# Queries projected three batches ahead in both attentions of a two-layer cross-attention kernel

## What is computed

```python
def _layernorm(x):
    m = jnp.mean(x, axis=-1, keepdims=True)
    v = jnp.var(x, axis=-1, keepdims=True)
    return (x - m) / jnp.sqrt(v + 1e-05)

# first attention, 16 heads of 16 numbers, no mask
q, k, v = heads(x0 @ Wq.T + bq), heads(ctx @ Wk.T + bk), heads(ctx @ Wv.T + bv)
out = softmax(-0.25 * q @ k.T) @ v                  # per head
attn0 = merge(out) @ Wp.T + bp
# second attention: rotary on queries and keys, and a mask
s = where(mask, neg, rope(q) @ rope(k).T)
attn1 = merge(softmax(s) @ v) @ Wo.T + bo

x = x + tanh(g_xattn[0]) * attn0(_layernorm(x), ctx)
x = x + tanh(g_ffn[0]) * ffn0(_layernorm(x))
x = x + tanh(g_xattn[1]) * attn1(_layernorm(x), ctx)
x = x + tanh(g_ffn[1]) * ffn1(_layernorm(x))
```

## Time and profile before

| | us |
|---|---|
| median of three runs | 790.41 |
| the profiled execution | 789.21 |
| its span, first to last instruction | 787.4 |
| TensorE busy | 682.1 (87%) |
| VectorE, ScalarE, GpSimd busy | 452.6, 334.4, 218.9 |
| step 0 of the first attention (30.82 to 44.72) | 13.90 |
| steps 1 to 5, each | 12.93 |
| steps 6 and 7 | 11.1 and 12.8 |
| step 8, the first of the second attention (to 387.00) | 24.4 |
| steps 9 to 12, each | 16.4 to 16.5 |
| steps 13, 14, 15 | 16.0, 11.5, 12.2 |

### The profile page before, as it was taken

How to read it: one execution, slowest core, us unless ns; L and a number is a source line. 1 busy time by engine, 2 the same in 40 slices (tenths; PEclk the granted TensorE clock), 3 DMA queues, 4 the chain that set the end, 5 groups by cost and what they waited for, 6 DMA issues and landing times.

```text
span 787.4 us, 13684 instructions
## 1 busy us (share of the span) xinstructions
PE 682.1 (87%) x5104; PEld 548.8 (70%) x5104; DVE 452.6 (57%) x919; ACT 334.4 (42%) x757; POOL 218.9 (28%) x200
## 2 busy tenths in 40 slices
PE   5889988999987637775999998999988899999998
PEld 4667655778864334443666665899976799999997
DVE  4758755110127465667467545545877777788713
ACT  3455655556641201113344555322227566555510
POOL 6635311000000500057254321000105545544500
PEclk9999999999998856998799999999999999999999
DMA  7865660670000223014334440400000455566313
GB/s 269 237 175 163 173 181 2 254 304 16 0 0 1 92 112 105 1 40 124 94 103 127 113 129 2 161 1 1 1 1 1 160 189 197 194 225 225 113 34 107
DMA packets 61479, 87.22 MB, mean 111 GB/s; under 512 B 17265, under 2 KB 50801, under 8 KB 60401
## 3 DMA queue, kind: packets, MB, share of 16 engines
q1 hardware_dynamic: 60624, 85.90, 34.1%
q10 hardware_dynamic: 800, 0.59, 0.2%
HBM read 63.54 MB, written 18.73 MB: 104 GB/s over the span
## 4 chain that ended last, share of the span: by engine, by line
PE 74%; DVE 11%; issue 6%; ACT 4%; POOL 3%; DMA 2%; ACTq 0%; DVEq 0%; POOLq 0%
PE ps L924 72%; DVE keep L1741 2%; DMA keep<-in_x 1%; ACT big L674 1%; DVE keep L1752 1%; PE ps L930 1%; POOL kbr L505 1%; ACT keep L684 1%; DVE keep L1734 1%; DVE keep L1749 1%; POOL vp L546 1%; PE ps L1400 1%; DVE mcol L1558 0%; DMA m_rows<-big 0%; ACT vp L674 0%
## 5 line engine op out<-in xcount | busy, mean ns | idle before, releaser
L924 PE MATMUL ps<-keep 128*128 128x120 bf16 (+9 forms) x517 | 83.9, 286 | 39.8 <-DVE keep L1741 30.8
L924 PEld LDWEIGHTS ps<-keep 128*128 128x128 bf16 (+2 forms) x517 | 42.2, 119 | 68.1 <-DVE keep L1741 43.8
L924 PE MATMUL ps<-thi,whi 128*128 128x256 f32 x256 | 73.8, 288 | 3.9 <-POOL tlo L603 2.1
L924 PE MATMUL ps<-thi,wlo 128*128 128x256 f32 x256 | 72.4, 283 | 0.0
L924 PE MATMUL ps<-tlo,whi 128*128 128x256 f32 x256 | 72.4, 283 | 0.0
L768 ACT ACTIVATE ps<-ps 128x256 f32<-128x256 f32 x128 | 47.6, 372 | 38.6 <-PE ps L924 38.6
L924 PE MATMUL ps<-qpair,kpair 98*77 98x256 f32 x256 | 57.9, 341 | 3.8 <-ACT big L674 2.2
L505 POOL TENSOR_TENSOR kbr<-khi,keep 128x616 fp32r<-128x616 f32 x32 | 40.9, 1300 | 65.9 <-PE ps L924 63.6
L837 ACT ACTIVATE att<-ps 128x512 f32<-128x512 f32 x48 | 28.6, 596 | 68.6 <-PE ps L924 68.3
L924 PE MATMUL ps<-xhi,phi 128*128 128x512 f32 x128 | 50.7, 396 | 2.9 <-ACT ps L768 2.9
L924 PEld LDWEIGHTS ps<-thi,whi 128*128 128x128 f32 x256 | 48.9, 191 | 5.8 <-issue 3.4
(11 more groups left out here) (219 smaller groups left out, 1812.0 us busy)
## 6 DMA issues: line engine op xcount, KB each, us to landing
qpair<-q_rows SPq DMA_DIRECT2D x16, 768.0 KB, 5.7
q_rows<-qhi SPq DMA_DIRECT2D x32, 256.0 KB, 2.7
big<-in_piw SPq DMA_DIRECT2D x4, 2048.0 KB, 12.4
q_rows<-qlo SPq DMA_DIRECT2D x16, 256.0 KB, 2.7
att<-in_wg SPq DMA_DIRECT2D x8, 512.0 KB, 3.6
att<-in_wu SPq DMA_DIRECT2D x8, 512.0 KB, 4.4
att<-in_wd SPq DMA_DIRECT2D x8, 512.0 KB, 5.2
big<-in_wg SPq DMA_DIRECT2D x8, 512.0 KB, 3.6
```

The lines of the kernel that those rows point to most:

```text
L924: return pe.matmul(out, lhsT, rhs, start=start, stop=stop, skip_group_check=True)
```

## The change

Batches are prepared earlier. Queries of batch `n + 3` are projected in step `n` (before: `n + 2`), the tokens of `n + 4` are transposed and copied (before: `n + 3`), and the statistics are those of `n + 5`. Step `lo` of each attention (0 and 8) does this twice over, in an order of its own, `attend_open`. In the other steps the row scores of `n + 2`, whose queries are a step old, come right behind the first key scores; the projection comes behind the second key scores; the transposes stand ahead of the last key scores. ScalarE's copy and rounding of turned tokens therefore stand ahead of `exponentials(n, (6, 7))`. In the second attention the output projection comes behind the first weighing. On SyncE the queries of batch 2 (10) leave ahead of the loop and those of `n + 3` in it. The waits follow: the output projection of `n - 1` waits until the low part of the queries of `n + 3` (first) or their first rotary product (second) has been read from bank 7.

Before, only the `TENSOR_SCALAR` of batch 4 stood between the two maxima. The diff, cut, SyncE first:

```diff
             def attend(layer):
+                queries_away(B * layer + 2)
                 for n in range(B * layer, B * layer + B - 2):
-                    queries_away(n + 2)
+                    if n + 3 < B * layer + B:
+                        queries_away(n + 3)
                     pair_keys(n + 2)
                     pair_queries(n + 2)
                     maxima_away(n + 2)
```

GpSimd:

```diff
+                if layer == 1:
+                    rotary_a(lo + 2)
+                inv_std(lo + 4)
                 for n in range(lo, hi):
-                    if n + 4 < hi:
-                        inv_std(n + 4)
-                    if layer == 1 and n + 2 < hi:
-                        rotary_a(n + 2)
-                    if n + 3 < hi:
+                    if n > lo and n + 3 < hi:
                         block_keys(n + 3)
+                    if n + 5 < hi:
+                        inv_std(n + 5)
+                    if n == lo:
+                        block_keys(n + 3)
+                    if layer == 1 and n + 3 < hi:
+                        rotary_a(n + 3)
```

ScalarE:

```diff
+                    first_queries = high_queries if layer == 0 else raw_queries
                     if n == lo:
+                        first_queries(n + 2)
                         maxima_out(n + 1)
+                        copy_xt(n + 3)
...
                     exponentials(n, (2, 3))
+                    if n == B:
+                        high_queries(n + 2)
+                    if n > lo and n + 3 < hi:
+                        first_queries(n + 3)
                     if n == 0:
                         values_out(3, PV_BANK + 1)
                     exponentials(n, (4, 5))
+                    if n == lo:
+                        first_queries(n + 3)
...
-                    if n + 2 < hi and layer == 1:
-                        high_queries(n + 2)
                     invert(n, 0)
-                    exponentials(n, (6, 7))
-                    if n + 3 < hi:
-                        copy_xt(n + 3)
+                    if n + 3 < hi and layer == 1:
+                        high_queries(n + 3)
+                    if n + 4 < hi:
+                        copy_xt(n + 4)
                     if n - 2 >= lo and layer == 0:
                         round_xt(n - 2, R_BANK + 1)
+                    exponentials(n, (6, 7))
                     if n + 2 < hi:
                         maxima_out(n + 2)
```

TensorE, its waits and its order:

```diff
                 if m % B > 1:
-                    pe.wait_ge(mT_done, m - (m % B == 2))
+                    pe.wait_ge(mT_done, m - 1)
+                if m % B == 3:
+                    if m < B:
+                        pe.wait_ge(qlo_done, m)
+                    else:
+                        pe.wait_ge(q_mulB, m - B)
...
-                    pe.wait_ge(qlo_done, min(n + 4, end))
+                    pe.wait_ge(qlo_done, min(n + 5, end))
                 else:
-                    pe.wait_ge(q_mulB, min(n + 4, end) - B)
+                    pe.wait_ge(q_mulB, min(n + 5, end) - B)
...
-                pe.wait_ge(xt_done, m + 1)
+                pe.wait_ge(xt_done, m + 1 if m % B < 2 else min(m + 2, B * (m // B + 1)))
...
+                if m % B == 2:
+                    if m < B:
+                        pe.wait_ge(qlo_done, m + 2)
+                    else:
+                        pe.wait_ge(q_mulB, m + 2 - B)
...
+            def attend_open(layer):
+                n = B * layer
+                key_scores(n, (0, 1))
+                project_q(n + 2)
+                maxima_to_rows(n + 1)
+                pe.wait_ge(max_done, 2 * n + 4)
+                transpose_xn(n + 3)
+                if layer == 0:
+                    project_values(PV_BANK + 1, 2)
+                key_scores(n, (2, 3))
+                if layer == 1:
+                    swap_pairs(n + 2)
+                else:
+                    pe.wait_ge(v_raw, 3)
+                    project_values(PV_BANK + 1, 3)
+                key_scores(n, (4, 5))
+                first_rows(n + 2)
+                project_q(n + 3)
+                weigh_values(n, 0)
+                second_rows(n + 2)
+                if layer == 1:
+                    swap_pairs(n + 3)
+                pe.wait_ge(max_done, 2 * n + 6)
+                transpose_xn(n + 4)
+                key_scores(n, (6, 7))
+                maxima_to_rows(n + 2)
+                if layer == 0:
+                    pe.wait_ge(v_raw, 4)
+                weigh_values(n, 1)
+
             def attend(layer):
                 lo, hi = B * layer, B * layer + B
-                for n in range(lo, hi):
+                attend_open(layer)
+                for n in range(lo + 1, hi):
                     m = n + 2
                     key_scores(n, (0, 1))
                     if m < hi:
-                        project_q(m)
-                    if n == lo:
-                        maxima_to_rows(n + 1)
-                    if n == 0:
-                        project_values(PV_BANK + 1, 2)
+                        if layer == 0 and m >= 5:
+                            pe.wait_ge(xlo_done, m - 4)
+                        first_rows(m)
                     key_scores(n, (2, 3))
+                    if n + 3 < hi:
+                        project_q(n + 3)
+                    key_scores(n, (4, 5))
                     if m < hi:
-                        if layer == 0:
-                            if m >= 5:
-                                pe.wait_ge(xlo_done, m - 4)
-                            first_rows(m)
-                        else:
-                            swap_pairs(m)
-                    if n == 0:
-                        pe.wait_ge(v_raw, 3)
-                        project_values(PV_BANK + 1, 3)
-                    key_scores(n, (4, 5))
-                    if n > lo:
+                        second_rows(m)
+                    if layer == 0:
                         project_out(n - 1)
-                    if m < hi:
-                        if layer == 0:
-                            second_rows(m)
-                        else:
-                            first_rows(m)
-                    weigh_values(n, 0)
-                    if m < hi and layer == 1:
-                        second_rows(m)
-                    key_scores(n, (6, 7))
-                    if n + 3 < hi:
+                        weigh_values(n, 0)
+                    else:
+                        if n + 3 < hi:
+                            swap_pairs(n + 3)
+                        weigh_values(n, 0)
+                        project_out(n - 1)
+                    if n + 4 < hi:
                         pe.wait_ge(max_done, 2 * n + 6)
-                        transpose_xn(n + 3)
+                        transpose_xn(n + 4)
...
+                    key_scores(n, (6, 7))
                     if m < hi:
                         maxima_to_rows(m)
```

VectorE in the first attention:

```diff
+                low_queries(2)
+                stats(4)
+                normalise(4)
+                stats(5)
+                maxima(2, 0)
+                low_queries(3)
+                normalise(5)
+                maxima(2, 1)
+                divide(0, 0)
+                for n in range(1, B):
+                    divide(n - 1, 1)
                     if n + 2 < B:
                         maxima(n + 2, 0)
-                    if n + 4 < B:
-                        normalise(n + 4)
-                    if n > 0:
-                        add_projection(n - 1)
+                    if n + 5 < B:
+                        stats(n + 5)
+                    if n + 3 < B:
+                        low_queries(n + 3)
+                    if n + 5 < B:
+                        normalise(n + 5)
                     if n + 2 < B:
                         maxima(n + 2, 1)
-                    if n > 0:
-                        stats_second(n - 1)
+                    add_projection(n - 1)
+                    stats_second(n - 1)
```

VectorE in the second attention:

```diff
+                rotary_b(10)
+                low_rotated(10)
+                stats(12)
+                normalise(12)
+                stats(13)
+                maxima(10, 0)
+                normalise(13)
+                maxima(10, 1)
+                rotary_b(11)
+                low_rotated(11)
+                divide(8, 0)
+                for n in range(B + 1, 2 * B):
+                    divide(n - 1, 1)
+                    if n + 2 < 2 * B:
+                        maxima(n + 2, 0)
+                    if n + 5 < 2 * B:
+                        stats(n + 5)
                     if n == 2 * B - 1:
                         split_shared(0)
+                    if n + 5 < 2 * B:
+                        normalise(n + 5)
                     if n + 2 < 2 * B:
-                        rotary_b(n + 2)
-                        low_rotated(n + 2)
-                    if n > B:
-                        add_projection(n - 1)
-                    if n + 2 < 2 * B:
-                        maxima(n + 2, 0)
-                    if n > B:
-                        stats_second(n - 1)
```

(12 more changed lines are left out.)

23 lines of the change are left out of this document (1 added, 22 removed).

## The result

The changed kernel takes 814.47 us (median of four runs, 806.39 to 822.66) against 790.92 for the kernel before on the same chip: ratio 1.0264, 95% interval 1.0177 to 1.0350. The kernel is slower, as forecast, but by 23.6 us where 7.6 was forecast, and outside the range; the interval puts the loss between 1.8 and 3.5%. The four runs spread as their mean granted clock does: 0.947 for the shortest, 0.927 for the longest. In all executions of the kernel before it lay between 0.950 and 0.959.

The account below looks back on a forecast made before the run. TensorE, its order fixed by hand, was taken to bound the kernel where that order stands still. Terms 6.6 + 0.4 + 5.4 + 0 - 4.8 = +7.6 us gave 798.0 us, own range 794.5 to 801.5, overall 791 to 805.

Parts of the forecast that it names:

- a rival of 0.15: First attention, steps 1 to 4: TensorE's clock falls once in each, up to +6.6 us more, 802 to 807; chance 0.15.
- step 0: First attention: second projection and transpose, a 2.6 us wait on the maxima of batch 2; +5.4 us.
- steps 1 to 4: First attention: 14.85 us for steps 2 and 3, 14.37 for 1 and 4, against 12.93; +6.6 us.
- steps 5 to 7: First attention: step 5 -0.6 without its projection, steps 6 and 7 +0.5 each from the rounding; together +0.4 us.
- step 8: Second attention's first step: row scores of batch 10 come 3 us earlier, but added work offsets it; 0 us.
- steps 9 to 15: Second attention: gains in steps 9 to 14, step 15 +1.1 from a later last division; sum -4.8 us.
- (b): First attention, steps 1 to 4: row scores leave the gap before the second key scores; projection starts at about s+2.37.
- (c): First attention, steps 1 to 4: output projection waits 1.1 us for the low queries in bank 7, starting at s+6.26.
- (d): First attention, steps 1 to 4: output projection, 1.82 us, stands right before the first weighing, which starts at s+8.08.
- (e): First attention: copy and rounding ahead of exponentials 6 and 7 each add 0.48 us before the second weighing.
- That the wait would be covered: Faster rival: output projection does not stand for low queries, transposes cost the exponentials nothing; 778 us, chance 0.08.
- that all would come out even: Rival: first attention's terms half as large (+6), second gaining 5; 791 to 793 us, chance 0.15 for 787 to 794.

Follow-up runs that it names:

- short fillings: Changed kernel with unread products (2, 2 and 6) sized to fit TensorE's waits before output projection, second weighing and step 0's transpose of batch 4: 807.34 us, ratio 1.0180.
- the run of this half alone: Kernel before with the changed order in the second attention alone, the first attention as before: 794.35 us, ratio 1.0036.
- before with (e) alone: Kernel before with, in the first attention, only transposes ahead of the last key scores and token copy and rounding ahead of the last exponentials: 800.44 us, ratio 1.0121.
- exponentials first: Changed kernel with last key scores and exponentials 6 and 7 again ahead of transposes, token copy and rounding in the first attention's steps 1 to 7: 807.81 us, ratio 1.0228.

## Why the forecast was right in sign and wrong in size

The step that failed is the clock: the sum put nothing for a lower clock and left it to a rival of 0.15. Measured, the changed kernel had 33.6 us more at the lower level, worth up to 16.8 of the 25.6 us. The waits were nearly right: with each stage put at full clock, as below, they come to +6.2 (step 0), +7.2 (steps 1 to 4), +0.6 (steps 5 to 7), -0.8 (step 8) and -4.2 (steps 9 to 15), 9.0 us for 7.6 forecast. That the waits draw the falls is shown inside the first attention, where shorter or filled waits took them away; of the falls outside it, one stands behind a wait that the change made longer, and the rest stays open.

**Steps 1 to 4: right.** (b), (c), (d) and (e) each came within 0.15 us of their distances. Steps 2 and 3 took 14.98 for 14.85, step 4 14.50 for 14.37. Step 1 took 15.28 for 14.37; 0.8 of the excess is the end of step 0's fall (with the short fillings it took 14.49).

**Step 0: the chain right, the size short.** The wait on the maxima was forecast at 2.6 us and was 3.06. From the transpose on the step took 6.39 us where the run with short fillings, at full clock there, took 4.22. Without that fall it would be 20.1, for 19.3 forecast.

**Steps 5 to 7: the term that was mis-sized is the clock.** Without falls they would have come near the forecast: step 5 took 12.56 for 12.3, step 6 would be 11.16 + 0.48 = 11.64, and took 13.27; from step 7 to the first feed-forward product it was 18.17 against 16.00 before, of which 0.5 is the wait. The forecast let the sum stand at full clock and priced the lower one as a rival of 0.15, on the argument that step 6 had run at full clock with the same busy share. That argument compared shares, and a share does not tell how the idle time lies. Step 6 of before had no wait over 1 us. In the changed kernel TensorE stands for 1.32 us in step 5 and 1.44 in step 6 before the second weighing, and the clock fell from 126.7 and from 140.4 us on, behind each, though it was busy 85% of step 5:

```profile
125.19 1.07 PE L935 MATMUL ps<-big,vp 77*32 77x256 f32 x16 [1.32 <-ACT big L681]
...
138.65 1.07 PE L935 MATMUL ps<-big,vp 77*32 77x256 f32 x16 [1.44 <-ACT big L681]
```

The rival was right in kind but mis-sized too: it looked for the falls in steps 1 to 4, where the first profile shows only the end of step 0's and the second two of 3.4 us, and only inside the attention. Its 803 to 805 are 10 us short.

The Trainium skill ("TensorE: Matmul & The Clock Gate", section "HAM oscillation — how this bites in real kernels") ties the lower clock to long gaps in which TensorE does nothing. No gap in steps 5 to 7 was longer than 1.5 us, so this case disagrees, as the earlier trace rows already did for step 7. The Trainium skill (same page, section "A second HAM failure mode: psum-queue depth-cycling") also describes a clock that swings under frequent short idling between groups of products; that is nearer to what is seen here.

**Second attention: most terms right, the ground wrong.** Steps 9 to 15 gained 4.2 us where the clock held, for 4.8: steps 9 and 10 gained nothing for 0.6 each, step 11 0.9, and steps 12 to 15 came within 0.3 us of their terms. Step 8 met its links: row scores, second row scores, transpose and last weighing came at s+8.2, 14.1, 17.7 and 21.4 in the run of this half alone, for 8.2, 14.4, 17.5 and 21.4 forecast, and it took 23.3, as forecast for full clock. But the term 0 was made against 24.1 us, and of four unfilled profiles of the old code two show 18.9, in which VectorE and GpSimd do not meet and the clock falls ahead of the wait. One profiled execution was taken as the kernel.

**Outside the attentions** the changed kernel lost 1.9 us at the start, 0.8 between and 5.0 behind, where 0 was forecast. The fall at the start (14 us) comes and goes with either code: the first key scores begin at 30.8 in the changed kernel profiled again, and at 32.4 in before with (e) alone. Behind the attentions 13.6 us were at the lower clock against 3.4 before, and the windows at 515 and 614 show where. The fall at 515 belongs to the change: it begins behind the wait of 2.18 us before the last output projection, and stands there in all nine profiles with the new second attention and in none of the five with the old. Where nothing else differs behind it (exponentials first), it makes the end 1.6 us longer. Some 90 to 100 us behind that projection, where the window at 614 lies, all fourteen profiles have a fall, with the old code too; it is longer in four of the nine, the changed kernel's two among them, and why is open. All five executions of the changed kernel have a lower mean clock (0.927 to 0.947) than any of before.

**Rivals.** That the wait would be covered, and that all would come out even, are refuted by the waits at 91.60 and 98.41 and by the total. SyncE cost nothing in the steps, as said: between the first key scores of an attention and its end no wait of TensorE over 0.2 us is ended by a DMA.

## What to carry to other kernels

Price a wait on TensorE at more than its length: in this kernel, whose clock fell here and there already, some 6.5 us of added waits cost 9.7 in their attention alone, in one profile, and 10.1 by the medians. When a forecast adds waits, read in the profile where the clock is already falling and put the fall into the sum, not among the rivals; and fill a wait with unread products once, as a test, to see how much of a loss is clock. Before a term is built on one large wait of one execution, look at that place in a second one, and at the whole profile too: here a stage of unchanged code differs by 3 us between two. And where two batches share a bank, moving the writer ahead moves the wait to the next reader.

## What was new about the hardware

The granted clock fell behind steps in which TensorE was busy 85% of the time and never stood longer than 1.5 us (step 5, then 0.76 in step 6), and stayed at 1.00 in the same steps when products filled two short waits nearly whole. A stretch of 6.8 us at the lower clock ahead of a wait left 1.42 us of that wait standing; one of 10.2 us behind it cost 4 us. And in two profiles a slower TensorE made another part come earlier: late by 1.5 us, it kept GpSimd's products from meeting VectorE's normalisation, which took 0.73 instead of 2.58 us.
